# A convolution stage with register loads one by one and a branch taken once

## The reference

```python
x = x + conv(_layernorm(x), block_values, cols, rows)    # block-sparse, causal
x = x + ffn(_layernorm(x), gate_w, w13, w2, sw13, sw2)   # 16 experts, top 6, and a shared one
x = x + attention(_layernorm(x), Wq, Wk, Wv, Wo, q_scale, k_scale)
x = x + ffn(_layernorm(x), gate_w, w13, w2, sw13, sw2)   # the same weights again
```

```python
x_unfold = xb[:, cols].reshape(batch, n_blocks * bs, t)
o = conv_general_dilated(x_unfold, W, padding=[(ks - 1, 0)], feature_group_count=n_blocks)
y = zeros(...).at[:, rows].add(o)
```

## Time and profile before

| what | value |
|---|---|
| median of 3 runs | 873.3 us (872.49 to 873.42) |
| the profiled execution | 872.59 us, of which its span is 870.8 us |
| TensorE busy | 857.7 us, 98% |
| VectorE busy | 514.8 us, 59% |
| mean granted clock of TensorE | 0.998 |
| the convolution stage | about the first 126 of the 870.8 us |

### The profile page before, as it was taken

One profiled execution on the slowest core, in us unless ns is written; L12 is line 12 of the kernel. 1 busy time (PEld: TensorE's weight loads), 2 busy tenths in 40 slices (PEclk: granted clock), 3 DMA queues, 4 the chain that ended last, 5 costly groups with the idle time before them and its releaser, 6 DMA issues.

```text
span 870.8 us, 16974 instructions
## 1 busy us (share of the span) xinstructions
PE 857.7 (98%) x5677; PEld 772.4 (89%) x5680; DVE 514.8 (59%) x1342; ACT 431.8 (50%) x1028; POOL 358.7 (41%) x334
## 2 busy tenths in 40 slices
PE   9999899999999999999999999999999999999998
PEld 7999778888888888799989998998997888888887
DVE  4888886333333338887688668768877433333334
ACT  4733425433434344776377557647746433434332
POOL 6754423656556563222121213212112555556552
PEclk9999999999999999999999999999999999999999
DMA  8999321111111102001000100000002111111111
GB/s 337 344 405 402 128 89 40 36 54 46 44 54 36 54 19 75 2 25 38 1 19 6 36 0 24 0 0 1 1 2 73 37 54 46 44 54 36 54 36 49
DMA packets 27859, 61.02 MB, mean 70 GB/s; under 512 B 3554, under 2 KB 11172, under 8 KB 27812
## 3 DMA queue, kind: packets, MB, share of 16 engines
q1 hardware_dynamic: 27812, 60.41, 20.0%
HBM read 59.35 MB, written 1.05 MB: 69 GB/s over the span
## 4 chain that ended last, share of the span: by engine, by line
PE 82%; DVE 10%; ACT 3%; issue 2%; DMA 2%; DVEq 0%; POOL 0%; ACTq 0%
PE bank L1269 29%; PE bank L1793 24%; PE bank L1282 14%; PE bank L1919 4%; DVE cv_acc L549 4%; PE bank L1859 3%; PE bank L1295 2%; PE bank L664 2%; PE bank L1305 2%; DMA cv_shared<-in_wtaps 2%; PE bank L1884 1%; ACT at_prob L1488 1%; DVE stats L74 1%; PE bank L648 1%; DVE xn L100 1%
## 5 line engine op out<-in xcount | busy, mean ns | idle before, releaser
L1168 DVE TENSOR_TENSOR f_h<-f_scaled,bank 128x512 f32<-128x512 f32 (+1 forms) x90 | 60.9, 676 | 179.4 <-POOL f_scaled L1033 166.9
L950 ACT ACTIVATE f_h_hi<-f_h 128x512 fp32r<-128x512 f32 (+2 forms) x102 | 63.6, 624 | 186.6 <-DVE f_h L1168 186.3
L1033 POOL TENSOR_TENSOR f_scaled<-f_act,f_gate_rows 128x512 f32<-128x512 f32 x80 | 103.0, 1288 | 116.1 <-ACT f_act L943 115.8
L1269 PE MATMUL bank<-f_xt_hi,f_w_lo 128*128 128x512 f32 x352 | 138.2, 393 | 0.0
L1269 PE MATMUL bank<-f_xt_hi,f_w_hi 128*128 128x512 f32 x352 | 137.8, 391 | 0.0
L1488 ACT ACTIVATE at_prob<-bank,at_sbias,at_qrs 128x512 f32<-128x512 f32 (+3 forms) x128 | 77.7, 618 | 72.4 <-DVE at_sbias L1680 72.4
L1175 DVE TENSOR_TENSOR f_h_lo<-f_h,f_h_hi 128x512 fp32r<-128x512 f32 (+2 forms) x102 | 71.8, 704 | 70.7 <-ACT f_h_hi L950 70.2
L1269 PE MATMUL bank<-f_xt_lo,f_w_hi 128*128 128x512 f32 x352 | 108.7, 390 | 0.0
L1282 PE MATMUL bank<-f_w_lo,f_h_hi 128*128 128x256 f32 (+1 forms) x352 | 99.6, 283 | 0.0
L1282 PE MATMUL bank<-f_w_hi,f_h_lo 128*128 128x256 f32 (+1 forms) x352 | 99.6, 283 | 0.0
L1282 PE MATMUL bank<-f_w_hi,f_h_hi 128*128 128x256 f32 (+1 forms) x352 | 99.3, 282 | 0.0
(11 more groups left out here) (254 smaller groups left out, 2127.5 us busy)
## 6 DMA issues: line engine op xcount, KB each, us to landing
cv_raw<-in_wconv SPq DMA_DIRECT2D x26, 512.0 KB, 7.6
cv_shared<-in_wtaps SPq DMA_DIRECT2D x32, 384.0 KB, 8.0
f_wraw<-in_w SPq DMA_DIRECT2D x42, 256.0 KB, 2.6
xn<-in_wconv SPq DMA_DIRECT2D x14, 512.0 KB, 7.2
f_wraw<-in_w SPq DMA_DIRECT2D x42, 128.0 KB, 2.5
at_wraw<-in_wqkv SPq DMA_DIRECT2D x3, 768.0 KB, 4.4
at_oraw<-in_wo SPq DMA_DIRECT2D x4, 512.0 KB, 3.5
X<-in_x_tiles SPq DMA_DIRECT2D x2, 512.0 KB, 7.9
```

The lines of the kernel that those rows point to most:

```text
L950: a.activation(h_hi[slot][0:rows, cols], h_f[half][0:rows, cols], ACT.Copy).then_inc(s["h_hi_done"], 1)
L1033: g.tensor_tensor(scaled[half][:], act[half][:], gate_rows[:, half * HALF:(half + 1) * HALF], ALU.mult).then_inc(s["scaled_done"], 1)
L1168: v.tensor_tensor(h_f[half][0:rows, cols], src[half][0:rows, cols], pu[half][0:rows, cols], ALU.mult)\
L1269: mm = t.matmul((pg, pu)[gu][half][0:out_rows, :], w, x, start=q == 0, stop=q == 3 * KH - 1)
```

## The change

VectorE loads one register at a time. Four are loaded ahead of the first block; then, between the two half additions of block i, the register of block i + 4 is loaded, up to block 127. TensorE branches on the flag once, ahead of the first sum, into one of two copies of its whole program: the straight one without the high products, the general one with them. Both copies include the three later stages. `LAST_PRODUCTS` is gone: `ADDED_ORDER`, itself reordered, now sets the order of TensorE too, and `LAST_OF` follows it. `convolve` holds the steps that stood in line before, from the first `sum_bank` to `convolve_added`, with `finish_products(st, general)`.

```diff
-OB, DB, PB, RING, DRING = 8, 4, 8, 6, 6
+OB, DB, PB, RING, DRING = 8, 4, 4, 6, 6
...
-        ADDED_ORDER = ((5, 0), (7, 0), (FIR + 2, 0), (5, 1), (FIR + 2, 1), (7, 1), (FIR + 3, 0), (6, 0), (FIR + 3, 1), (6, 1))
-        LAST_PRODUCTS = ((5, 0), (FIR + 2, 0), (FIR + 2, 1), (FIR + 3, 0), (FIR + 3, 1), (6, 0), (7, 0), (5, 1), (6, 1), (7, 1))
-        LAST_OF = ((FIR + 3, 1), (7, 0), (7, 1))
+        ADDED_ORDER = ((5, 0), (7, 0), (FIR + 2, 0), (FIR + 2, 1), (FIR + 3, 0), (FIR + 3, 1), (6, 0), (5, 1), (7, 1), (6, 1))
+        LAST_OF = ((FIR + 3, 1), (6, 0), (6, 1))
...
-            def load_pairs(d):
+            def load_pair(i):
                 return nc.values_load_multi_w_load_instructions(
-                    line_pair[0:1, d * PB:(d + 1) * PB], engines=[mybir.EngineType.DVE], min_val=0, max_val=NW - 1,
-                    skip_runtime_bounds_check_because="columns and rows are numbers of channel blocks, 0 to 7 each")[1]
+                    line_pair[0:1, i:i + 1], engines=[mybir.EngineType.DVE], min_val=0, max_val=NW - 1,
+                    skip_runtime_bounds_check_because="columns and rows are numbers of channel blocks, 0 to 7 each")[1][0]
 
             def add_block(i, pairs):
+
+                at = pairs.pop(i)
...
-                    dst = acc[:, :, bass.ds(pairs[i % PB], 1), part].rearrange("p e a f -> p e (a f)")
+                    dst = acc[:, :, bass.ds(at, 1), part].rearrange("p e a f -> p e (a f)")
...
                     add.then_inc(s["added"], 1)
+                    if k == 0 and i + PB < NBLK:
+                        pairs[i + PB] = load_pair(i + PB)
...
-            pairs = load_pairs(0)
+            pairs = {i: load_pair(i) for i in range(PB)}
...
-            for i in range(2, PB):
+            for i in range(2, NBLK):
                 add_block(i, pairs)
-            for p in range(1, NBLK // PB):
-                pairs = load_pairs(p)
-                for i in range(p * PB, (p + 1) * PB):
-                    add_block(i, pairs)
...
-        def tensor(t):
-
+        def tensor(t, following_program):
...
-            def finish_products(st):
+            def finish_products(st, general):
                 t.wait_ge(s["ws_lo_done"], rounded(st, SB - 1))
-                with t.If(flag != 0):
+                if general:
...
-                for n, (f, r) in enumerate(LAST_PRODUCTS):
+                for n, (f, r) in enumerate(ADDED_ORDER):
...
-                    if n == len(LAST_PRODUCTS) - 1:
+                    if n == len(ADDED_ORDER) - 1:
...
+            def convolve(general):
...
+
+            with t.If(flag == 0):
+                convolve(False)
+                following_program(t)
+            with t.Else():
+                convolve(True)
+                following_program(t)
...
-            conv[4](t)
-            ffn1[4](t)
-            attention[4](t)
-            ffn2[4](t)
+            def after_convolution(t):
+                ffn1[4](t)
+                attention[4](t)
+                ffn2[4](t)
+
+            conv[4](t, after_convolution)
```

More of the change, by code:

```diff
@@ L750, in tensor @@
             flag = t.value_load(any_high[0:1, 0:1], min_val=0, max_val=1)
[L751 to L773, removed]
+            def convolve(general):
+                for st in range(2):
+                    for q in range(SB):
+                        sum_bank(st, q)
+                t.wait_ge(s["ws_lo_done"], SB)
+                t.wait_ge(s["xc_lo_done"], 4 * B)
+                for u in units(0):
+                    products(*u)
+                finish_products(0, general)
+                sum_and_convolve(2, paced(1))
+                finish_products(1, general)
+                first = [units(FIR, slice(4 * i, 4 * i + 4)) for i in range(2)] + [[]] * (SB - 2)
+                sum_and_convolve(3, [a + b for a, b in zip(first, paced(2))])
+                finish_products(2, general)
+                sum_and_convolve(4, paced(3))
+                finish_products(3, general)
+                t.wait_ge(s["ws_lo_done"], rounded(FIR + 1, 0))
+                for u in units(FIR + 1):
+                    products(*u)
+                t.wait_ge(s["ws_lo_done"], rounded(NPE - 1, SB - 1))
+                for u in units(4):
+                    products(*u)
+                finish_products(4, general)
+                convolve_added()
+            with t.If(flag == 0):
[4 more added lines that the diff above has]
+                following_program(t)
     def ended(e):
```

## The result

| | before | after | ratio, 95% interval |
|---|---|---|---|
| median | 872.89 us (872.12 to 873.42, 4 runs) | 892.01 us (890.58 to 893.47, 4 runs) | 1.021 (1.0186 to 1.0234) |
| profiled execution | 872.59 us | 892.73 us | |
| its span | 870.8 us | 890.9 us | |

The account below looks back on a forecast made before the run. VectorE's additions were taken to bound the convolution, each microsecond counting in the kernel. They would end at 143.3 us against 101.1, +42.2, less 0.6 for Part 2: +41.6 on 872.6 gives 914.0 us, range 884 to 932.

Parts of the forecast that it names:

- the price of a load of one: On VectorE's queue: 0.49 us, taken from TensorE's load of a single register, between bounds 0.075 and 0.598.
- start: Ahead of VectorE's first addition: four single loads take 2.40 us in place of 0.89, so additions begin at 38.7 us.
- a block: VectorE's queue per block: load 0.49, gap 0.05, two additions at 0.13, together 0.80 us; 124 blocks make 99.2 us.
- GpSimd's long subtractions: VectorE stands during two of them, 2.38 us each; taken as 4 us in all, with short ones disappearing in spare time.
- a load stops the queue: VectorE's queue does nothing else while it loads; only a half addition already handed over, 0.17 us, runs beside it.
- Part 2: TensorE's two program versions and new product order: five branches go, costed at a gain of 0.6 us, bounds 0 and 2.9.
- The jump at the end: Program's end, over the general copy: may take 3 us from TensorE's end, covered by the output transfer within a few tenths.
- The clock: TensorE idles longer before the added products and starts them at 1.2 GHz in place of 2.4, costing 0 to 1 us.
- TensorE's busy share: Sign of being right: from 37 to 143 us, during VectorE's additions, it falls to some 60%.
- partly covered or shorter (0.25 to 0.42 us): Rival on VectorE's loads: the wait slot lets the queue run further ahead; 884 to 905 us, chance 0.11.
- The likeliest rival: On VectorE's queue, a load of one costs as much as eight, 0.60 us; block 0.91, time 928, chance 0.17.
- the faster rival: VectorE's loads vanish, the queue going on or a load under some 0.15 us; gain 4 to 6 us, 868, chance 0.12.

Follow-up runs that it names:

- second_flag: The kernel before with TensorE's flag loaded twice in a row and the registers' sum tested; second load 0.309 us, kernel run once at 879.27 us.
- register_per_half: The changed kernel with a register of its own for each half of a block, two loads of one behind every first half; 936.31 us, ratio 1.0711.
- behind_second: The changed kernel with each load behind the second half addition of its block instead of the first; 891.03 us, ratio 1.0204.
- clock_kept: The changed kernel with three more matmuls of zeros ahead of TensorE's wait for each of banks 16 to 39; 891.10 us, ratio 1.020.
- program_only: The changed kernel with the loads of eight put back, leaving only TensorE's one branch and new orders; 874.19 us, ratio 1.0019.
- loads_only: The kernel before with only VectorE's single loads; TensorE's program and both orders as before; 892.38 us, ratio 1.0211.
- branch_only: The kernel before with only the one branch and the two program copies; orders and loads of eight as before; 873.13 us, ratio 1.0001.
- two_a_load: The changed kernel with two registers per load, behind the first half of every second block; 890.69 us, ratio 1.0194.

## Why the prediction was right or wrong

**The step that failed** is the price of a load of one: "It is the same operation with the same count, on another engine's queue, so I take 0.49." It measured 0.301 us. That the queue stands still for a load was right; the size of the term was not, and it was taken 124 times. Operation and queue were no difference, as second_flag shows; the row was a first load. The trace of before had this in sight: VectorE's first load of eight took 0.843 against a median of 0.598, and the forecast used the 0.24 us between them for the start of the additions and not for TensorE's row. Less 0.24, the row gives 0.25 us, near 0.30. The sum with the right price, by the forecast's own steps (the gap behind a load in a block measured 0.035 us, not 0.05):
- start: four loads of 0.35 and the 0.25 of the first make 1.65 in place of 0.89, so 37.96 us; measured 37.94;
- a block: 0.30 + 0.035 + 2 x 0.13 = 0.595 us; measured 0.59; 124 of them 73.8 us;
- the last four 1.4, GpSimd's long subtractions 4: 117.2 us; measured 119.64.

The forecast's 143.3 was thus 23.7 too late, of which 124 x 0.205 = 25.4 is the price (0.80 a block against 0.595), 0.8 the start, and about 2.5 the other way: 6.5 us are left over for GpSimd, not 4. The blocks beside its two long subtractions took 2.74 and 2.80 us in place of 0.59, which is 4.4; most of the other blocks that took longer lie beside its short ones. I had let those disappear in the spare time of a block, but at 0.59 us a block leaves 0.25 us to spare, not 0.46.

The measured time lies inside the forecast's range, 884 to 932, and that is no credit to it: the range was drawn wide enough to take in the rivals, and the forecast's own lengths of a load were 0.42 to 0.56 us.

**Right:** that a load stops the queue. It was read from one wait recorded at 37.0, and register_per_half (44 us for 124 more loads) bears it out; behind_second (no change) fits it. Also right: VectorE is the chain and TensorE is not (clock_kept, program_only); a microsecond of additions is one of the kernel (18.6 us, and behind them the tail of 25.4 us unchanged; 43.6 against 43.4 us in register_per_half). The later stages were forecast to keep their length; they took 1.5 us more.

**Part 2**, forecast as a gain of 0.6 us within 0 to 2.9, gave none; alone it costs 1.2 us: 1.0019 (1.0010 to 1.0028). VectorE's wait took the stalls' place, as said. Beside the slow additions it does have a use that I didn't see: it saves TensorE 1.07 + 2.59 us at a place where TensorE is late (loads_only), of which 2.6 us show in the length of that kernel's tail. The medians, 892.38 and 892.01, don't resolve it, and 1.6 us of it were given back later. The jump at the end was costed rightly: the branch lasts 3.829 us from 886.0, to 889.8, and SyncE's queue still waits for the last output transfer until 890.6. Whether the slower issue of that transfer, 0.5 us, has to do with the branch is open; in program_only and branch_only, with the same branch at the end, it was issued only 0.05 us slower than before. The two rows:

```profile
L775 PEldq COMPARE_BRANCH  x2: 92/1960/3829, 7.1 to 886.0; - x2
```

```profile
L2044 SPq COMPARE_BRANCH  x1: 38/38/38, 890.6 to 890.6; - x1
```

The Trainium skill, "Runtime: NRT & Kernel Launch", section "Instruction fetch mechanics": by its rule on taken branches, the branch that falls through (0.092 us) and the one that leaves for distant code (3.829 us) differ as they do here. The trace agrees with it. Loads of one, two and four registers took 0.301, 0.526 and 0.344 us here. The Trainium skill, "DMA: Bandwidth & Descriptors", section "Latency and other measured facts", has a floor of about 600 ns for a tensor load; the measurements decide, and it does not hold for these three.

**The clock** was forecast to cost 0 to 1 us ahead of the added products. It fell earlier and for longer, from about 74 to 118 us, and that was free; the second fall, from 145.4 to 148.8 us, cost about 1 of the unforecast 1.5 us behind the additions. TensorE's busy share was forecast to drop to some 60%, with over 30 us of cover between the issue of its last bank and the additions' end. The last bank was issued at 94.9, 24.7 us ahead of that end, but at half the clock TensorE stayed busy without a break from 74 to 118 us and used the cover up: it was ready at 121.7, when VectorE's first subtraction (120.48 + 1.14 = 121.62) had just let it go. That it cost nothing was close; in loads_only TensorE came too late.

**The rivals.** The one that comes nearest is the second, "partly covered or shorter (0.25 to 0.42 us)", given 0.11 and 884 to 905 us. Its reason, that the queue runs further ahead, was wrong; the load was shorter. The likeliest rival, a load as dear as one of eight (0.60), fell with the 0.301. No part of the faster rival held.

## What to carry to other kernels

A register load stopped VectorE's whole queue here, and of its 0.30 us 0.25 were paid, though it stood beside an addition. What counts is the number of loads times the measured length of one, and not the number of registers: one of eight cost 0.55 us, eight of one 8 x (0.59 - 0.34) = 2.0 us, four of two 4 x (1.14 - 0.68) = 1.8 us, and two of four 2 x (1.64 - 1.36) = 0.6 us. Before a price is taken from a single row, look whether that row is the first load on its queue: another kind's first against its median tells the surcharge. And when one chain is slowed, an engine beside it may lose its clock, and what that costs depends on where it falls: 44 us of it cost nothing here while TensorE was off the chain, 3.4 us of it cost 1 us where TensorE was on it. Add work to keep the clock before blaming it.

## What the runs showed that I had not expected

- The price of a load by its registers on VectorE: 1: 0.301, 2: 0.526, 4: 0.344, 8: 0.598, 16: 1.106 us. Four cost less than two.
- A queue's first load is dearer, by 0.24 to 0.26 us on VectorE whatever the number of registers: 0.554 against 0.301 (one), 0.785 against 0.526 (two), 0.595 against 0.344 (four), 0.843 against 0.598 (eight), 1.347 against 1.106 (sixteen); on TensorE 0.497 against 0.309 us (one).
- TensorE's granted clock stayed at 1.2 GHz for 44 us of continuous matmuls (about 74 to 118 us; the mean of 70 to 80 us is 0.68, of 80 to 118 us 0.50). Ahead of it stood a wait of 0.66 us for a bank in which transfers had come later:

```profile
72.75 2.85 PE L662 MATMUL bank<-cv_onehot,xn 128*128 128x64 f32 x16 [0.66 <-DMA xn<-in_wconv]
```

- No kernel here beat the one before. Four registers a load stay 2 us above it by the medians, which the interval does not quite tell from no change; sixteen give nothing, with the transfers as the next wait.
- What a stretch at 1.2 GHz costs at the start of the feed-forward stage. From the last normalization's start to TensorE's last matmul's end, the eight traces without one have 740.9 to 741.5 us, the five with one of 3.4 us 741.9 to 742.3, and two_a_load, with one of 6.8 us, 743.1.
